# The attention pass of a graph network: two more of its six groups scattered as three bf16 parts, the weighing and the scores in one operation each, the codes' copy on ScalarE

## What is computed

```python
h = (x @ W).reshape(n, HEADS, CH)
e = leaky_relu(a_src[src] + a_dst[dst], 0.2)
e = exp(e - m[dst])                                  # m: highest score of a node's edges
out = segment_sum(h[src] * (e / segment_sum(e, dst)[dst])[:, :, None], dst)
```

## Time and profile before

| | |
|---|---|
| median of 3 runs | 4967.69 us (4963.65 to 4969.53) |
| the profiled execution, its own time | 4966.04 us |
| its span | 4964.2 us |
| busy: PE, DVE, ACT, POOL | 4459.2, 4111.3, 2873.8, 801.3 us |
| attention pass in the span | from 1033 to about 1992 us |

### The profile page before, as it was taken

The page is one execution under the profiler, slowest core; times in us unless marked ns, Lnnn a source line. Parts: engine busy times, 40 slices in busy tenths (PEclk is TensorE's granted clock), DMA queues, the critical chain, the costliest instruction groups (busy, mean ns, idle before and its releaser), DMA issues.

```text
span 4964.2 us, 254617 instructions
## 1 busy us (share of the span) xinstructions
PE 4459.2 (90%) x101536; PEld 4017.0 (81%) x101536; DVE 4111.3 (83%) x6842; ACT 2873.8 (58%) x9065; POOL 801.3 (16%) x1001
## 2 busy tenths in 40 slices
PE   1999999669999999499969999969999998999998
PEld 1677777469999999488869999958888886888887
DVE  7799999889999999888888989977767776767676
ACT  1999999512222222477743333356666665666665
POOL 2455555311111111000012222200000000000000
PEclk7999999879999999799979999989999999999999
DMA  1000000068887887000024444433333333333333
GB/s 53 2 1 2 2 1 2 17 191 254 255 253 252 255 254 231 14 0 0 0 64 121 121 119 121 117 82 98 99 96 98 98 96 92 101 98 100 99 99 83
DMA packets 305222, 501.40 MB, mean 101 GB/s; under 512 B 76918, under 2 KB 78454, under 8 KB 305126
## 3 DMA queue, kind: packets, MB, share of 16 engines
q1 hardware_dynamic: 303782, 499.39, 34.6%
q0 software_dynamic: 576, 0.52, 0.1%
q10 hardware_dynamic: 768, 0.16, 0.0%
HBM read 408.40 MB, written 91.57 MB: 101 GB/s over the span
## 4 chain that ended last, share of the span: by engine, by line
PE 51%; issue 17%; DVE 15%; ACT 12%; POOL 3%; DMA 1%; DVEq 1%; ACTq 0%; POOLq 0%; SPq 0%
PE PS L1514 19%; ACT arena L863 11%; PE PS L1507 9%; PE PS L1311 7%; PE PS L1289 5%; PE PS L1291 5%; DVE arena L1823 4%; DVE arena L2467 3%; POOL arena L792 2%; PE PS L1306 2%; PE PS L1545 1%; PE PS L1443 1%; PE PS L1428 1%; PE PS L1318 1%; DVE arena L2393 1%
## 5 line engine op out<-in xcount | busy, mean ns | idle before, releaser
L1823 DVE TENSOR_TENSOR arena<-iotab,arena 128x1024 bf16<-128x1024 bf16 (+3 forms) x1887 | 1749.2, 960 | 228.1 <-PE PS L1514 167.7
L1040 ACT ACTIVATE arena<-PS 128x384 bf16<-128x384 f32 x2450 | 1001.4, 498 | 543.2 <-PE PS L1507 543.2
L1514 PE MATMUL PS<-arena 32*128 32x193 bf16 (+1 forms) x41552 | 994.8, 242 | 44.6 <-DVEq L2468 41.1
L1514 PEld LDWEIGHTS PS<-arena 32*128 32x128 bf16 x41552 | 838.3, 92 | 149.5 <-DVEq L2468 58.0
L863 ACT ACTIVATE arena<-PS,m 128x196 bf16<-128x196 f32 x1813 | 739.7, 448 | 21.7 <-PE PS L1148 21.7
L1507 PE MATMUL PS<-Hp,arena 128*128 128x192 bf16 (+1 forms) x4900 | 536.5, 248 | 35.8 <-DVE Hp L1667 35.4
L1289 PE MATMUL PS<-Hp,arena 128*128 128x72 bf16 x7350 | 500.0, 198 | 43.9 <-DVE arena L2169 40.3
L1020 ACT ACTIVATE arena<-PS,ewB 128x64 f32<-128x64 f32 x1176 | 257.4, 330 | 420.6 <-PE PS L1351 420.6
L1291 PE MATMUL PS<-arena 128*128 128x72 bf16 x7350 | 500.6, 198 | 0.0
L1507 PEld LDWEIGHTS PS<-Hp,arena 128*128 128x128 bf16 x4900 | 382.1, 99 | 145.9 <-issue 84.9
L1155 PE MATMUL PS<-arena,tmp 128*128 128x262 bf16 x1813 | 450.8, 277 | 17.0 <-DVE tmp L1823 14.8
(11 more groups left out here) (376 smaller groups left out, 7954.6 us busy)
## 6 DMA issues: line engine op xcount, KB each, us to landing
arena<-hots SPq DMA_DIRECT2D x735, 256.0 KB, 2.6
arena<-codes SPq DMA_DIRECT2D x245, 512.0 KB, 5.1
hots<-arena SPq DMA_DIRECT2D x245, 256.0 KB, 5.2
arena<-hots SPq DMA_DIRECT2D x147, 320.0 KB
arena<-codes SPq DMA_DIRECT2D x49, 640.0 KB, 5.6
hots<-arena SPq DMA_DIRECT2D x49, 320.0 KB, 5.5
rows_h<-Hn SPq DMA_DIRECT2D x4, 1568.0 KB, 9.8
rows_l<-Y SPq DMA_DIRECT2D x1, 1764.0 KB, 9.8
```

Of the source, the lines that this page charges most:

```text
L1040: act.activation(RG[ROW_BUFFER[g]][:, 2 * i:2 * i + 2, 0:RW], ps[PAIR_BANK[q]][:, 0:2 * RW].rearrange("p (k c) -> p k c", k=2), ACT.Copy). ...
L1514: last = pe.matmul(ps[2 + q][:, b * SW:b * SW + SW - o], one_hot[32 * q:32 * q + 32, b * P:(b + 1) * P], rows_of[32 * q:32 * q + 32, 0:SW ...
L1823: return dve.tensor_tensor(to.rearrange("p k (n t) -> p k n t", t=4), iota_of[:, 0:n].rearrange("p (n t) -> p n t", t=4)[:, None, :, :] .t ...
```

## The change

- Groups with g % 3 = 1 (groups 1 and 4) are scattered in parts, as those with g % 3 = 0 are. There is a second buffer W3 for their parts, a `rest` and a `lowest_part` for each, and no f32 one-hots. Whole are now groups 2 and 5 alone, with one buffer OD and one Wf.
- `weigh` is one operation over both banks of a group, and so is the reduce of `scores`.
- The copy `cdw` is made by ACT, in two halves (`slot_codes`), one after groups 0 to 2 are compared and one after groups 3 to 5.
- `evict` has no wait for its own operation; the semaphore's increment is attached to it. The second one waits for the first one's count.

```diff
-        OD = [None] + [cv.take(GS[1] * P).rearrange("p (k n) -> p k n", n=P) for _ in range(2)]
+        OD = cv.take(GS[2] * P).rearrange("p (k n) -> p k n", n=P)
...
-        W3 = cv.take(GS[0] * PARTS * WV).rearrange("p (k a c) -> p k a c", a=PARTS, c=WV)
+        W3 = [cv.take(GS[a] * PARTS * WV).rearrange("p (k a c) -> p k a c", a=PARTS, c=WV) for a in range(2)]
...
+        def scored(g):
+
+            a = turn_of(g)[0]
+            return PS[:, a * 512:(a + 2) * 512].rearrange("p (h x) -> p h x", h=2)[:, :, 0:GS[g] // 2 * WIDE] \
+                .rearrange("p h (k c) -> p h k c", c=WIDE)
...
+        def in_parts(dx, g):
+
+            return dx * 4 + (g // 3 * 2 + g % 3 + 1)
...
                 def lowest_part(dx, g):
-                    pool.wait_ge(p_rest, dx * 2 + (g // 3 + 1))
-                    pool.tensor_tensor(W3[:, 0:GS[g], 2, :], W3[:, 0:GS[g], 1, :], W3up[:, 0:GS[g], 1, :],
+                    pool.wait_ge(p_rest, in_parts(dx, g))
+                    a, n = g % 3, GS[g]
+                    pool.tensor_tensor(W3[a][:, 0:n, 2, :], W3[a][:, 0:n, 1, :], W3up[a][:, 0:n, 1, :],
                                        ALU.subtract).then_inc(p_low, 1)
...
                 with pool.Fori(1, LASTW) as d:
                     lowest_part(d, 0)
+                    lowest_part(d, 1)
                     table_of(d + 1)
                     lowest_part(d, 3)
+                    lowest_part(d, 4)
...
-                if g % 3:
+                if g % 3 == 2:
                     act.wait_ge(f_ohb, dx * NG + g + 1)
                     act.wait_ge(f_scat, dx * NG + g + 1)
-                    act.activation(OD[g % 3][:, 0:GS[g], :], ODb[g % 3][:, 0:GS[g], :], ACT.Copy).then_inc(f_ohd, 1)
+                    act.activation(OD, ODb[2], ACT.Copy).then_inc(f_ohd, 1)
+
+            def slot_codes(to, dx, h, seen):
+
+                if not is_zero(dx):
+                    act.wait_ge(f_ohb if seen is None else f_ohd, dx * NG + ((seen or 0) - 3 + 3 * h))
+                cols = slice(0, HALF) if h == 0 else slice(HALF, CPW)
+                act.activation(to[:, cols, :], cdA3[:, bass.ds(dx, 1), cols].rearrange("p w c -> p (w c)")
+                               [:, :, None].to_broadcast((P, cols.stop - cols.start, 4)), ACT.Copy).then_inc(f_codes, 1)
...
                     for g in range(NG):
+                        if g % 3 == 2 and not last:
+                            slot_codes(cdw, dx + 1, g // 3, None)
...
-                if g % 3 == 0:
-                    pe.wait_ge(p_low, dx * 2 + (h + 1))
+                if g % 3 < 2:
+                    pe.wait_ge(p_low, in_parts(dx, g))
                     pe.wait_ge(f_ohb, n + 1)
...
                 else:
                     pe.wait_ge(f_whole, n + 3)
-                    pe.wait_ge(f_ohd, dx * 4 + (2 * h + g % 3))
+                    pe.wait_ge(f_ohd, dx * 2 + (h + 1))
...
                 def one_hots(dx, g):
-                    if g == 0:
-                        if not is_zero(dx):
-                            dve.wait_ge(f_ohb, dx * NG)
-                        flink(dve.tensor_copy(cdw, fours(cdA3[:, bass.ds(dx, 1), :].rearrange("p w c -> p (w c)"))))
                     if g % 3 == 0:
+                        dve.wait_ge(f_codes, dx * 2 + (g // 3 + 1))
+                    if g % 3 < 2:
                         dve.wait_ge(f_scat, dx * NG + (g + 1))
...
                 def scores(dx, g):
                     dve.wait_ge(f_gath, dx * NG + g + 4)
-                    m = GS[g] // 2
-                    for h in range(2):
-                        last = dve.tensor_reduce(
-                            mx[g % 2][:, h * m:(h + 1) * m, :],
-                            scored_half(g, h)[:, :, DIM:WIDE].rearrange("p k (a c) -> p k c a", a=2), AX.X, ALU.max)
-                    last.then_inc(f_mx, 1)
+                    dve.tensor_reduce(mx[g % 2][:, 0:GS[g], :].rearrange("p (h k) c -> p h k c", h=2),
+                                      scored(g)[:, :, :, DIM:WIDE].rearrange("p h k (a c) -> p h k c a", a=2),
+                                      AX.X, ALU.max).then_inc(f_mx, 1)
...
+                    dve.tensor_tensor(
+                        weighed(g)[:, :, 0:DIM].rearrange("p (h k) (n c) -> p h k n c", h=2, n=HEADS),
+                        scored(g)[:, :, :, 0:DIM].rearrange("p h k (n c) -> p h k n c", n=HEADS),
+                        weighed(g)[:, :, DIM:WV].rearrange("p (h k) n -> p h k n", h=2)[:, :, :, :, None].to_broadcast(to),
+                        ALU.mult).then_inc(f_whole, 1)
...
                         dve.wait_ge(f_sum, dx + 1)
+                        dve.wait_ge(f_accout, dx * 2 + 3)
                     to = agg[:, bass.ds(dx, 1), 0:WV].rearrange("p w c -> p (w c)")
-                    flink(dve.tensor_tensor(to, to, ps[4 + h][:, 0:WV], ALU.add))
-                    dve.sem_inc(f_accout, 1)
+                    dve.tensor_tensor(to, to, ps[4 + h][:, 0:WV], ALU.add).then_inc(f_accout, 1)
...
-                        if g % 3 == 0:
+                        if g % 3 < 2:
                             rest(dx, g)
```

More of the change, by code:

```diff
@@ L314, in gnn_stack @@
         ODb = [cv.take(GS[a] * P, bf16).rearrange("p (k n) -> p k n", n=P) for a in range(3)]
-        OD = [None] + [cv.take(GS[1] * P).rearrange("p (k n) -> p k n", n=P) for _ in range(2)]
+        OD = cv.take(GS[2] * P).rearrange("p (k n) -> p k n", n=P)
         WV = DIM + HEADS
-        Wf = [None] + [cv.take(GS[1] * WV).rearrange("p (k c) -> p k c", c=WV) for _ in range(2)]
-        W3 = cv.take(GS[0] * PARTS * WV).rearrange("p (k a c) -> p k a c", a=PARTS, c=WV)
-        W3up = W3.rearrange("p k a c -> p (k a c)").bitcast(bf16).rearrange(
-            "p (k a c t) -> p k a c t", a=PARTS, c=WV, t=2)[:, :, :, :, 1]
+        Wf = cv.take(GS[2] * WV).rearrange("p (k c) -> p k c", c=WV)
+        W3 = [cv.take(GS[a] * PARTS * WV).rearrange("p (k a c) -> p k a c", a=PARTS, c=WV) for a in range(2)]
+        W3up = [v.rearrange("p k a c -> p (k a c)").bitcast(bf16).rearrange(
+            "p (k a c t) -> p k a c t", a=PARTS, c=WV, t=2)[:, :, :, :, 1] for v in W3]
         mx = [cv.take(GS[0] * HEADS).rearrange("p (k c) -> p k c", c=HEADS) for _ in range(2)]
@@ L458, in turn_of @@
             return ((0, 1), (2, 3), (6, 7))[g % 3]
[L460 to L462 removed]
+        def scored(g):
+            a = turn_of(g)[0]
+            return PS[:, a * 512:(a + 2) * 512].rearrange("p (h x) -> p h x", h=2)[:, :, 0:GS[g] // 2 * WIDE] \
+                .rearrange("p h (k c) -> p h k c", c=WIDE)
         def weighed(g):
[L466 removed]
+            return Wf if g % 3 == 2 else W3[g % 3][:, 0:GS[g], 0, :]
+        def in_parts(dx, g):
+            return dx * 4 + (g // 3 * 2 + g % 3 + 1)
         block = ctx.enter_context(nc.Block())
@@ L747, in _ @@
                 lowest_part(0, 0)
+                lowest_part(0, 1)
                 pool.wait_ge(f_mg, 16 * 2 * MC)
@@ L752, in _ @@
                 lowest_part(0, 3)
+                lowest_part(0, 4)
                 pool.wait_ge(f_mexp, 1)
@@ L760, in _ @@
                     lowest_part(d, 0)
+                    lowest_part(d, 1)
                     table_of(d + 1)
                     lowest_part(d, 3)
-                lowest_part(LASTW, 0)
-                lowest_part(LASTW, 3)
+                    lowest_part(d, 4)
+                for g in (0, 1, 3, 4):
+                    lowest_part(LASTW, g)
             pool.wait_ge(s_table, 16 * 3)
@@ L942, in _ @@
             with act.Else():
+                for h in range(2):
+                    slot_codes(cdw, 0, h, None)
                 exponents(0, 0)
@@ L1299, in scatter @@
                 to = ps[4 + h][:, 0:WV]
-                if g % 3 == 0:
-                    pe.wait_ge(p_low, dx * 2 + (h + 1))
+                if g % 3 < 2:
+                    pe.wait_ge(p_low, in_parts(dx, g))
                     pe.wait_ge(f_ohb, n + 1)
-                    pe.wait_ge(f_accout, dx * 2 + (h + 1))
+                    if g % 3 == 0:
+                        pe.wait_ge(f_accout, dx * 2 + (h + 1))
                     for k in range(GS[g]):
                         for a in range(PARTS):
-                            last = pe.matmul(to, ODb[0][:, k, :], W3up[:, k, a, :], start=(k == 0 and a == 0), stop=False)
+                            last = pe.matmul(to, ODb[g % 3][:, k, :], W3up[g % 3][:, k, a, :],
+                                             start=(g % 3 == 0 and k == 0 and a == 0), stop=False)
                 else:
                     pe.wait_ge(f_whole, n + 3)
-                    pe.wait_ge(f_ohd, dx * 4 + (2 * h + g % 3))
+                    pe.wait_ge(f_ohd, dx * 2 + (h + 1))
                     for k in range(GS[g]):
-                        last = pe.matmul(to, OD[g % 3][:, k, :], Wf[g % 3][:, k, :], start=False,
+                        last = pe.matmul(to, OD[:, k, :], Wf[:, k, :], start=False,
                                          stop=(g == 2 and k == GS[g] - 1))
@@ L2195, in weigh @@
```

(9 more changed lines are left out.)

14 lines of the change are left out of this document (5 added, 9 removed).

## The result

The changed kernel takes 4879.3 us (median of 4 runs, 4870.5 to 4890.2) against 4965.8 us before (median of 4: the three runs of the table and one more); the ratio is 0.9828, 95% interval 0.9816 to 0.9841. The profiled execution took 4874.5 us, its span is 4872.6.

A forecast was written before the change was run, and what follows sets the result against it. PE bounds the kernel before; after the change DVE does, at 15.98 + 1.72 = 17.70 us a window against PE's 17.29. (19.39 - 17.70) x 49 = 83 us, less 1 for the last window: 4966 - 82 = 4884 us, range 4861 to 4930.

The forecast's parts named there:

- PE's part: Attention pass: two scatters a window go from 1.81 to 0.76 us, so PE's window falls from 19.39 to 17.29 us.
- DVE's part without contention: Attention pass: DVE's window, added up without losses at the port shared with POOL, falls from 19.39 to 15.98 us.
- the 1.5 us by which PE would have stayed the bound: DVE's window: saving of twelve operations at the Trainium skill's 125 ns overhead each, against 0.73 us from the profile rows.
- The race: Behind each rest, compare and POOL's lowest part compete for the port; the compare, 0.03 us ahead, wins all four times.
- the border lies near 0.03: Compare against POOL's lowest part: a compare starting up to about 0.03 us after POOL's record still gets through.
- The rival's price, all four lost: Rival: all four compares are blocked by POOL, DVE's window is 19.71 us and the kernel 4982 us; chance 0.14.
- the contention: DVE's losses at the port shared with POOL: 1.72 us a window, raising DVE's window from 15.98 to 17.70 us.
- step 3: Group 3's step in a window: few stands right behind the compare, is blocked by POOL's lowest part and loses 0.83 us.
- the rival in which PE stays the bound: Attention pass: PE still sets the time at 17.29 us a window, the kernel takes 4863 us; chance 0.16.
- The sum: Whole kernel: 49 windows save 83 us, less 1 us for the last window; 4966 - 82 = 4884 us.
- The transfers: Buffer reloads, 5.1 us of landing, stay hidden unless landing grows over 1.4 us; rival with 0.3 beyond: 4912 us, chance 0.06.
- The small waits of PE for POOL and DVE: Attention pass after the change: PE shows small waits for POOL's lowest part and for DVE; scatter 4 waits 0.4 us.

The follow-up runs named there:

- No_parts: Kernel before with all of the change except the bf16 parts; groups 1 and 4 stay whole: 4965.0 us, ratio 0.9999.
- parts_alone: Kernel before with only groups 1 and 4 scattered in bf16 parts; weighing, scores, codes and linked sums as before: 5021.6 us, ratio 1.0113.
- pe_less: Changed kernel with the gather leaving out the lowest part of the table of targets, 50 of 300 matmuls a window: 4887.2 us, ratio 0.9834.
- few_parts_late: Changed kernel with the few edges' scatter in three bf16 parts, few left at its place: 4882.5 us, ratio 0.9832.
- again: Changed kernel run once more, nothing altered: 4870.5 us, ratio 0.9797.
- two_reduces: Changed kernel with only the merged reduce of the scores undone, two reduces again: 4945.6 us, ratio 0.9946.

## Why the prediction was right, and where it was not

**PE's part**: right. Two scatters of 1.81 us became 0.76 each, and the sum of 17.29 us was measured as 17.28.

**DVE's part without contention**: right within 0.1 us. After, the losses at the port are 0.46 (L2194 behind group 1's compare), 0.21, 0.48 and 0.23, together 1.38, and 17.28 - 1.38 = 15.90 against 15.98. The merged reduce takes 0.13 us, the merged weighing 0.60, the unlinked sum 0.14 with nothing at the loop's end, as estimated from other passes. The twelve operations saved bring some 0.07 us each, 0.84 in all; the 1.5 us by which PE would have stayed the bound are not borne out. No_parts shows that this part alone is worth nothing and parts_alone that without it the kernel is slower: 0.9999 and 1.0113.

**The race**: the direction right, the border too plain. All compares won once one reduce brought them 0.01 to 0.04 us ahead, mostly 0.02. But "the border lies near 0.03" holds at most for the place it was read from: behind rest 0 of the kernel before, four compares won at 0.032 to 0.036 us after POOL and 45 lost at 0.035 to 0.040. With two reduces, at 0.04 and 0.05 us behind, the compares behind rests 0 and 4 win in 48 of 49 windows and those behind rests 1 and 3 lose in 48 or 49. In parts_alone the compares behind rest 1, all 0.04 us behind, win 26 times and lose 23 times. The rival's price, all four lost, was 19.71 us; undoing the reduce alone gave 18.74.

**The failed step** is in the contention, at step 3: "behind the compare stands few (L2219), with two SBUF inputs, at once: 0.83 lost", and with it "So DVE becomes the bound, by 0.4 us". Few lost nothing, the L2194 after it lost 0.48, DVE's window came to no more than PE's, and the rival in which PE stays the bound describes the steady state. I had walked one window in the order of DVE, let table_of come as early as PE could be there, and so priced few as if POOL's lowest part always started right behind the rest. In the kernel it stands behind table_of, which waits for a gather of PE (4.64 us, and 9.34 already in the earlier trace rows), and starts 1.26 us after the compare. Where table_of is not in the way, the price was right: in the last window, which has none, few takes 1.45 us in the changed kernel itself, and pe_less and few_parts_late sit at 17.65 us a window with few at 1.44, once PE is faster. Whether the changed kernel could stay in that state from another start is open; its two profiles show it in no window of the loop.

**The sum**: the forecast, 4884, is 5 us above the median and 10 above the profiled run. So small a distance is luck. Two errors partly cancel: the window was 0.42 us too long (19 us), and nothing was set aside for the start, where the profiled run lost 7.8 us in its second window. The same kernel without that loss (again) saves 101 us on its chip, where the forecast was 82 and the rival with PE as the bound 103.

**The transfers**: the landing of a reload is 5.1 us after as before, at a DMA share of 0.89 in place of 0.79 to 0.82; in the steady state DVE waits for none. The small waits of PE for POOL and DVE that the prediction named do not come up: PE has none from 1100 to 1850 us. In the last window it waits 1.1 us for POOL, where the sum had 1.

## What to carry to other kernels

When one engine is relieved by loading the one behind it, add up the second engine's whole window, with the losses at what it shares, and ask at each shared port which two operations meet there after the change. An engine without idle time is not yet a bound: make it work a little more, or the other a little less, and see whether the period moves. Where a wait is decided by a few hundredths of a microsecond, change the order so that no race is left; here that, one operation moved and the few edges in parts took a window from 17.28 to 16.88 us (ratio 0.9797 and 0.9765).

## What the runs showed of the hardware that I had not expected

- The same distance in the records, 0.04 us, goes one way in one place and the other way in another (two_reduces, 48 of 49 windows or more), and both ways in one place (parts_alone, 26 and 23). The recorded starts alone do not tell who gets the port.
- Less work on the bound engine made the pass longer twice: 1.63 us less gave 17.65 instead of 17.28 us a window, 0.39 us less the same 17.65.
- Near the start of the pass PE can stand for up to 3.1 us with no releaser in the profile, and the granted clock then falls from 2.4 to 1.2 GHz. The DMA share does not explain it: from 1033 to 1053 us it is 0.93 both in the first profile and in again, which has no such gap. All eight gaps end 1.2 to 1.5 us after a 16 KB block of the queue named "instruction".
